# Two heads' exponentials in one ScalarE instruction on the narrow causal tiles and in each layer's last head group

## What is computed

```python
# layer 0: 32 heads of 16, T = 1024, causal; an adapter of 10 keys is added to y
q, k, v = split(x @ w_attn.T); q = rope(q); k = rope(k)
scores = einsum('bhqd,bhkd->bhqk', q, k) / sqrt(16)
attn = softmax(where(causal, scores, -inf))
y = einsum('bhqk,bhkd->bhqd', attn, v)
# layer 1: the same with 8 key heads, each shared by 4 query heads, own rope base
```

## Time and profile before

| | us |
|---|---|
| median of 3 runs | 1012.19 |
| the three runs | 1011.4, 1012.19, 1014.52 |
| profiled execution, its time | 1011.6 |
| profiled execution, span of the trace | 1009.9 |
| attention of layer 0, first to last result copy | 179.87 to 400.47 |
| attention of layer 1, first to last result copy | 605.40 to 827.52 |
| granted TensorE clock, mean (1 is 2.4 GHz) | 0.938 |

### The profile page before, as it was taken

One profiled execution on the slowest core, in us unless ns is written; L12 is line 12 of the kernel. 1 busy time (PEld: TensorE's weight loads), 2 busy tenths in 40 slices (PEclk: granted clock), 3 DMA queues, 4 the chain that ended last, 5 costly groups with the idle time before them and its releaser, 6 DMA issues. The chain is left out here.

```text
span 1009.9 us, 15158 instructions
## 1 busy us (share of the span) xinstructions
PE 915.9 (91%) x5334; PEld 503.2 (50%) x5334; DVE 669.6 (66%) x1177; ACT 503.5 (50%) x1134; POOL 278.4 (28%) x527
## 2 busy tenths in 40 slices
PE   6887989999999998988698599999999889799997
PEld 4555853433444432855365233434444338577766
DVE  5975547877788760965748577877778518455464
ACT  5221322776766665224612146777767652367630
POOL 2454141223223321033345122223223212013200
PEclk9997985999999999988789779999999999899999
DMA  9332060221212110200023400111100010321001
GB/s 323 94 95 79 1 149 25 55 53 54 65 49 63 47 40 7 99 1 1 0 75 112 111 22 25 37 40 39 41 26 2 2 42 1 136 82 64 22 32 53
DMA packets 50029, 57.14 MB, mean 57 GB/s; under 512 B 8928, under 2 KB 39712, under 8 KB 49952
## 3 DMA queue, kind: packets, MB, share of 16 engines
q1 hardware_dynamic: 48320, 55.75, 18.4%
q10 hardware_dynamic: 1632, 0.39, 0.2%
HBM read 43.41 MB, written 12.32 MB: 55 GB/s over the span
## 5 line engine op out<-in xcount | busy, mean ns | idle before, releaser
L1001 DVE TENSOR_REDUCE mx<-psum 128x1 f32<-128x512 f32 (+3 forms) x640 | 370.6, 631 | 114.5 <-PE psum L866 70.1
L861 PE MATMUL psum<-arena_s 96*128 96x512 bf16 (+3 forms) x768 | 226.5, 349 | 9.6 <-DVE mx L1001 5.5
L947 ACT ACTIVATE arena_p<-psum 128x512 f32<-128x512 f32 (+1 forms) x384 | 185.1, 591 | 92.7 <-PE psum L886 61.6
L886 PE MATMUL psum<-arena_s 99*128 99x512 bf16 (+3 forms) x768 | 204.4, 335 | 8.5 <-ACT arena_p L947 3.3
L947 ACT ACTIVATE arena_x<-psum 128x128 f32<-128x128 f32 (+2 forms) x384 | 133.9, 439 | 88.6 <-PE psum L886 65.7
L861 PEld LDWEIGHTS psum<-arena_s 96*128 96x128 bf16 x768 | 71.2, 99 | 124.4 <-DVE mx L1001 70.9
L886 PEld LDWEIGHTS psum<-arena_s 99*128 99x128 bf16 x768 | 66.9, 98 | 100.9 <-ACT arena_p L947 34.4
L1052 POOL TENSOR_SCALAR_AFFINE_SELECT arena_p<-arena_p 128x256 f32<-128x256 f32 x128 | 50.9, 408 | 204.2 <-ACT arena_p L947 204.2
L259 PE MATMUL psum<-x_h,w 128*128 128x512 f32 x224 | 87.9, 456 | 10.8 <-DVE w L476 7.6
L866 PE MATMUL psum<-maskb,ident_b 128*128 128x128 bf16 (+1 forms) x384 | 96.5, 251 | 0.0
L904 PE MATMUL psum<-arena_p,v_grp 128*32 128x512 f32 (+1 forms) x768 | 91.5, 597 | 0.0
(11 more groups left out here) (202 smaller groups left out, 1203.6 us busy)
## 6 DMA issues: line engine op xcount, KB each, us to landing
q_parts<-arena_p SPq DMA_DIRECT2D x48, 128.0 KB
arena_s<-q_parts SPq DMA_DIRECT2D x32, 192.0 KB, 2.9
arena_s<-k_parts SPq DMA_DIRECT2D x96, 64.0 KB, 2.3
ff_raw<-in_w_in SPq DMA_DIRECT2D x11, 512.0 KB, 3.6
arena_s<-q_parts SPq DMA_DIRECT2D x32, 128.0 KB, 3.0
k_parts<-arena_p SPq DMA_DIRECT2D x30, 128.0 KB
arena_w<-in_w SPq DMA_DIRECT2D x12, 256.0 KB, 6.5
ff_wd_raw<-in_w_down SPq DMA_DIRECT2D x1, 2560.0 KB, 11.3
```

What stands on the lines that cost most here:

```text
L861: last = pe.matmul(psum[:, bank, width * n:width * n + width], q_st[0:KS, b % NS, 512 * r + P * i:512 * r + P * i + P], k_st[0:KS, g % NK, ...
L886: pe.matmul(psum[:, 2 * (n % 2) + t, o:512], k_st[0:KM, g % NK, at:at + P], q_st[0:KM, u % NS, 512 * r + o:512 * r + 512], start=True, sto ...
L947: act.activation(pr[n % NP_RING][:, t, o:512], psum[:, 2 * (n % 2) + t, o:512], ACT.Exp, scale=scale).then_inc(exp_ready, 1)
L1001: dve.tensor_reduce(mx[:, b % 2, kc, col:col + 4 * len(heads) - 3:4], src, AX, ALU.max)\
```

## The change

Where the tile is 256 or 128 columns wide (`o >= 256`), and on every tile of units 14 and 15 (`u >= NU - CH`), the two heads of a pair are taken by one instruction that reads both banks. It waits for the scores of both heads, and both `exp_ready` counts are given when it ends. Other tiles keep an instruction for each head. Nothing else is changed.

```diff
@@ -942,6 +942,12 @@
                 o = first_column(steps[u][0], b // 2)
                 if n >= NP_RING:
                     act.wait_ge(pv_done, 2 * ((n - NP_RING) // 2) + 2)
+                if o >= 256 or u >= NU - CH:
+                    act.wait_ge(scores_ready, 2 * n + 2)
+                    act.activation(pr[n % NP_RING][:, :, o:512],
+                                   psum[:, 2 * (n % 2):2 * (n % 2) + 2, o:512],
+                                   ACT.Exp, scale=scale).then_inc(exp_ready, 2)
+                    return
                 for t in range(2):
                     act.wait_ge(scores_ready, 2 * n + t + 1)
                     act.activation(pr[n % NP_RING][:, t, o:512], psum[:, 2 * (n % 2) + t, o:512],
```

## The result

| | before | changed |
|---|---|---|
| median of the runs of the first comparison | 1012.08 us (4 runs) | 1020.51 us (4 runs) |
| ratio, 95% interval | | 1.0073 (1.0037 to 1.0109) |
| two more comparisons of 12 runs each | 1014.86 (35 runs), 1014.96 (26 runs) | 1019.77, 1019.57 |
| their ratios | | 1.0053 (1.0031 to 1.0075), 1.0049 (1.0024 to 1.0074) |
| span of the trace | 1009.9 | 1014.7 |

The first comparison has the changed kernel 8.4 us slower, the two larger ones 4.9 and 4.6, where 2.1 us were forecast; in the means of the larger ones it is about 5 us, half a per cent. The first four runs of the kernel before were quick ones (mean 1012.5, against 1015.0 over 128 later runs). The measured time of 1020.5 lies 6.2 us above the forecast of 1014.3 and outside its range of 1011.8 to 1017.6.

What follows compares the result with a forecast made beforehand. A wait loop between TensorE and ScalarE in the last head groups, not ScalarE's rate, was taken as the bound. Terms of 1.16 us (layer 0) and 0.95 (layer 1) made +2.1, so 1014.3 us; range 1011.8 to 1017.6.

Steps and rivals of the forecast that it cites:

- Where TensorE waits for ScalarE, and where not: Middle groups, units 0 to 13, keep TensorE fed and stay at 29.23 us; only the last group has it waiting.
- The price of a merge, 0.06 us: One exponential for two heads saves ScalarE 0.06 us against two; a 512-column pair takes 1.03 us alone.
- rival B: Each merge saves 0.17 us, not 0.06, on six chain merges a layer, giving 1013.0 us; chance 0.11.
- The round: Full-width two-tile round of unit 15, S(3', p1) to S(5', p1), grows from 4.73 to 4.99 us: +0.27 a layer.
- Unit 14 and the start of unit 15: Later score products cost 0.14 us a layer in unit 14, then 0.65 in layer 0 and 0.44 in layer 1.
- The first term: In unit 14, S(3, p0) waits for merged E(2, p0), its second head one short product later: +0.14 us a layer.
- First tiles of unit 14 at 0 under cover: Delay of S(1, p0) costs 0, hidden by a 1.84 us mask wait; without that wait 0.3 us a layer.
- Behind attention everything follows in order, so the delay is passed on whole.: The 2.1 us lost in the two attentions reaches the total time undiminished, with nothing added after them.
- rival A: Further half-clock stretches of TensorE in the last groups, +1.7 us each: 1016.0 us with one, 1017.7 with two; chance 0.30.
- The base: Starting time for the forecast: the median of three runs of the kernel before, 1012.2 us.
- D: Middle groups lose 0.10 us in each narrow passage, +1.4 us in all, giving 1015.7 us; chance 0.06.
- the first case: The forecast itself, 1014.3 us, at chance 0.47; a sixth of it, with its open terms, lay beyond 1015.2 us.

Runs made afterwards that it cites:

- e3: Changed kernel with two-head exponentials kept only on the 256- and 128-column tiles of units 0 to 13; mean 1016.3 us, ratio 1.0009 to the kernel before.
- e4: Kernel before, one exponential for each head, plus the change's waits for both heads in all its places; mean 1020.9 us, ratio 1.0059.
- f1: The change on top of e8; median 1011.74 us, ratio 0.9978 to the kernel before.
- e6: Kernel before with two-head exponentials in units 14 and 15 of layer 1 alone; mean 1017.2 us, ratio 1.0022.
- g4: e4 measured a second time without any edit; mean 1021.5 us, ratio 1.0052 to the kernel before.
- g3_changed_third: The changed kernel measured a third time without any edit; median 1019.57 us, mean 1020.0 us.
- e8: Kernel before with GpSimd's split of the last unit's maxima put one mask later; median 1010.28 us, ratio 0.9927.

## Why the prediction was wrong, point by point

- **Where TensorE waits for ScalarE, and where not.** Right. Middle groups at 29.23 us, no difference in e3.
- **The price of a merge, 0.06 us.** Right, or a little low: 1023 ns against 1.03 us, and the changed kernel has 0.49 and 0.41 a layer less than e4, where six merges at 0.06 make 0.36 and at rival B's 0.17 would make 1.0. Rival B is out.
- **The round.** Right: 5.00 measured, 4.99 forecast. ScalarE's idle time in it was forecast at 1.2 and came out at 1.34.
- **Unit 14 and the start of unit 15.** From unit 13's copy to unit 15's layer 0 became longer by 1.17 where 1.16 stood; layer 1 by 1.15 (9.50 + 16.27 against 8.81 + 15.81) where 0.95 stood. The first term left out the copy of unit 13's result, which now comes 0.13 later in each layer behind a merged pair. Sum 2.6 instead of 2.1.
- **First tiles of unit 14 at 0 under cover.** Right, and f1 shows the price without it: 0.45 instead of 0.3.
- **"Behind attention everything follows in order, so the delay is passed on whole."** Taken by itself this holds: 2.5 us of pure delay cost 2.9. The step that failed is what the sum made of it: everything outside the walked places was put at no change. The walked delay, 2.6 us, is only about half of the loss of 5. An estimated 1.3 to 1.7 us more come with 6 us more half-clock time. The prediction had half clock as rival A, but at one kind of place, inside the last groups, as a matter of 0.30 that either happens or not. In the three traces of the changed kernel the last groups have as much of it as before (6.8 us each), and the excess lies in stretches where no line was changed; a further stretch inside the last groups, as rival A had it, shows once each in e6 and g4. About a us of the 5 is explained by neither term and is the size of the errors of the means. That the serial waits bring the whole loss is shown by e4 and g4; how they bring the part outside the last groups stays open.
- **The base.** The largest part of the miss of 6. The forecast was set on 1012.2, the median of three runs, and on a trace with 125 us of half clock. 128 later runs of the same kernel gave a mean of 1015, and none of them had under 135. So the trace that I read was from the quick end, and 2.8 us of the miss are that. The three runs were 3 us apart, which should have widened the range upwards, as should the stretches before and between the attentions, where the mean clock of 0.938 had room to differ (in later runs of the kernel before it was 0.922 to 0.933, and once 0.887).
- **Direction.** The chance for slower by over 0.3% was 0.42 and for no difference 0.54. The weights were on the wrong side because two terms were left out that only add: the half clock outside the last groups, and unit 13's later copy. The error of the base moves both kernels alike and has no part in this.
- **Slips in the working.** The parts named for "slower" (A, D and a sixth of the first case) make 0.44, where 0.42 stands, and A with its second stretch, 1017.7, lies just above the range said to take it in. Neither changes the outcome.

## What to carry to other kernels

An instruction for two items saves one fixed cost, here about 0.06 us, and makes both neighbours wait for the later item: where the buffer between two engines is two deep, count the serial work that appears on both sides of the merge before counting instructions. The test that settled it is cheap: put the merged form's waits on the old instructions, and the two effects stand apart. Where an engine shows long waits in a round, a deeper ring was worth 0.9 us a round, and one mask moved ahead of a blocked instruction 6.8 us in the two layers together; of layer 0's 3.6, nearly half was clock that the wait had cost behind it. And a forecast for a kernel whose runs differ by 10 us needs more than three runs as its base.

## What the runs showed of the hardware that I had not expected

- Runs of one kernel differ by up to 14 us (1013.0 to 1027.2 for g3_changed_third), and the difference goes with TensorE's half-clock time: 135 to 170 us of it in the kernel before and those with merges or waits alone, but for one run of the kernel before at 231, and 0.22 to 0.28 us of time for each. The part ahead of layer 0's first result copy had 37.5 us of it in one trace of the kernel before, where it took 178.2 us, and 58 in that of e8, which has the same code there, where it took 186.1.
- A wait of 1.84 us of TensorE cost twice its length: in the traces of the kernel before there is half clock in the unit behind it in both layers, and none there in those of e8 and f1, where the wait is gone. The Trainium skill (TensorE: Matmul & The Clock Gate, "HAM oscillation — how this bites in real kernels") tells of waits of TensorE for transfers, behind which the next products run at the lower clock. This case's traces agree in kind, with a wait for a mask: unit 14 of layer 0 went from 0.64 to 1.00 of full clock.
- An exponential over two PSUM banks costs what its columns cost: 1023 ns for 1024, against 994 for a copy of 1024 columns, and with 256 columns of each bank 605 ns, against 623 for one of 512 columns in one bank.
